# The score tiles of a step start with head 0 of their own key tile, and the copy of the finished values moves one exponential later

## What is computed

```python
# x (4, 512, 256), ctx_768 (4, 1601, 192); 16 heads of 16
q = (layernorm(x) @ Wq + bq).reshape(B, N, 16, 16)
k = (ctx @ Wk + bk).reshape(B, M, 16, 16)
v = (ctx @ Wv + bv).reshape(B, M, 16, 16)
attn = softmax(einsum('bnhd,bmhd->bhnm', q, k) / 4)
out = einsum('bhnm,bmhd->bnhd', attn, v).reshape(B, N, 256)
x = x + tanh(g_xattn) * (relu(out @ W1 + b1) @ W2 + b2)
x = x + tanh(g_ffn) * moe(layernorm(x))     # shared expert + top 2 of 8
```

## Time and profile before

| | |
|---|---|
| median of 3 runs | 1040.58 us (1040.33 to 1040.69) |
| the profiled execution | 1041.95 us, its span 1039.9 us |
| TensorE busy | 1021.9 us of the span |
| VectorE busy | 672.5 us |
| ScalarE busy | 610.9 us |
| attention steps | from about 61 us to about 720 us |
| granted TensorE clock, mean of the span | 0.997 of full speed |

### The profile page before, as it was taken

One profiled execution on the slowest core, in us unless ns is written; L12 is line 12 of the kernel. 1 busy time (PEld: TensorE's weight loads), 2 busy tenths in 40 slices (PEclk: granted clock), 3 DMA queues, 4 the chain that ended last, 5 costly groups with the idle time before them and its releaser, 6 DMA issues. The chain is left out here.

```text
span 1039.9 us, 15726 instructions
## 1 busy us (share of the span) xinstructions
PE 1021.9 (98%) x5777; PEld 555.7 (53%) x5777; DVE 672.5 (65%) x915; ACT 610.9 (59%) x1144; POOL 208.5 (20%) x217
## 2 busy tenths in 40 slices
PE   8899999999999999999999999999999999999998
PEld 6434445344445433444543353333676888888865
DVE  4998786896787798578788668711488222222326
ACT  3167777876677777577777768774365222222211
POOL 6129200009000003600000021020002233333310
PEclk9999999999999999999999999999999999999999
DMA  8263030430302402203033030011591111111207
GB/s 217 73 168 64 1 64 7 122 64 1 63 13 52 115 16 60 52 13 63 2 63 64 2 63 1 22 57 45 171 335 31 36 52 51 52 51 51 52 26 242
DMA packets 38281, 70.15 MB, mean 67 GB/s; under 512 B 6848, under 2 KB 23360, under 8 KB 38208
## 3 DMA queue, kind: packets, MB, share of 16 engines
q1 hardware_dynamic: 33072, 57.88, 21.3%
q0 software_dynamic: 3744, 10.23, 3.3%
q10 hardware_dynamic: 1392, 1.05, 0.4%
HBM read 33.70 MB, written 9.31 MB: 41 GB/s over the span
## 5 line engine op out<-in xcount | busy, mean ns | idle before, releaser
L1041 DVE TENSOR_REDUCE mpart<-gu_ps 128x2 f32<-128x1024 f32 x384 | 456.8, 1221 | 83.5 <-PE gu_ps L891 83.4
L743 ACT ACTIVATE probs<-ring_ps 128x512 f32<-128x512 f32 x816 | 433.1, 598 | 125.5 <-PE ring_ps L906 118.4
L906 PE MATMUL ring_ps<-qst,kst 64*128 64x512 f32 x816 | 224.8, 461 | 2.8 <-ACT probs L743 2.1
L921 PE MATMUL pv_ps<-probs,vp 128*32 128x512 f32 (+2 forms) x1664 | 222.7, 604 | 0.6 <-ACT osb L677 0.6
L906 PEld LDWEIGHTS ring_ps<-qst,kst 64*128 64x128 f32 x816 | 98.5, 180 | 207.6 <-ACT probs L743 117.8
L891 PE MATMUL gu_ps<-kst,qst 63*128 63x512 f32 (+1 forms) x1024 | 178.4, 396 | 6.6 <-DVE mpart L1041 5.4
L891 PEld LDWEIGHTS gu_ps<-kst,qst 63*128 63x128 f32 x1024 | 91.9, 186 | 66.7 <-DVE mpart L1041 42.3
L1261 ACT ACTIVATE h_sb<-gu_ps 128x512 f32<-128x512 f32 x55 | 32.8, 596 | 134.8 <-PE gu_ps L1415 134.7
L1468 DVE TENSOR_TENSOR h_sb<-h_sb,gu_ps 128x512 f32<-128x512 f32 x55 | 37.8, 687 | 113.3 <-ACT h_sb L1261 112.8
L302 POOL TENSOR_SCALAR veps<-mv 128x4 f32<-128x4 f32 x8 | 1.8, 231 | 531.9 <-DVE mv L1010 282.8
L1435 PE MATMUL y_ps<-wd,hT 128*128 x312 | 73.8, 380 | 0.0
(11 more groups left out here) (223 smaller groups left out, 1187.5 us busy)
## 6 DMA issues: line engine op xcount, KB each, us to landing
kst<-parts SPq DMA_DIRECT2D x45, 401.0 KB, 5.6
qst<-parts SPq DMA_DIRECT2D x48, 128.0 KB, 4.5
wgu<-in_WgT SPq DMA_DIRECT2D x16, 256.0 KB, 8.5
wgu<-in_WuT SPq DMA_DIRECT2D x16, 256.0 KB, 8.4
wd<-in_WdT SPq DMA_DIRECT2D x8, 512.0 KB, 9.6
wgu<-picked SPq DMA_DIRECT2D x8, 512.0 KB, 7.4
cold<-in_ctxT SPq DMA_DIRECT2D x3, 800.5 KB, 4.2
cold<-in_ctxT SPq DMA_DIRECT2D x6, 400.2 KB, 5.9
```

The costliest lines, as they stand in the source:

```text
L743: nc.scalar.activation(probs[0:w, m % NPB, h, :], bank_of(("st", idx))[0:w], ACT.Exp, scale=SCALE).then_inc(exp_done, 1)
L906: nc.tensor.matmul(bank_of(("st", idx))[0:w], kst[u % NKB][rows, h // 2, mt * P:mt * P + w], qst[u % NKB][rows, h // 2, :], start=True, st ...
L921: last = nc.tensor.matmul(pv_ps[32 * h:32 * h + c1 - c0, :], values[:, c0:c1], probs[0:w, m % NPB, h, :], start=(mt == 0), stop=(mt == MT ...
L1041: nc.vector.tensor_reduce(mpart[:, :, p, t, q], s_ps[:, n % NSP], AX.X, ALU.max).then_inc(s_free, 1)
```

## The change

The score tiles of a step become heads 0, 1, 2 and 3 of its own key tile, so each head 3 moves from the start of a step to the end of the one before. `lead` is 2 in every step. In unit 15 nothing is shifted beyond its first step: there the tiles ran one further ahead already, and still do. `take_pv` moves from the end of ScalarE's work in step mt = 0 to a place after the first exponential of step mt = 1. Ring and engines follow the same lists.

```diff
+LEADING = 2
...
-        first, last = (2 if m > MT * (UNITS - 1) else 0), (2 if m >= MT * (UNITS - 1) else 0)
-        return list(range(max(4 * m - 1 + first, 0), min(4 * m + 3 + last, 4 * MT * UNITS)))
+        first, last = (1 if m > MT * (UNITS - 1) else 0), (1 if m >= MT * (UNITS - 1) else 0)
+        return list(range(4 * m + first, min(4 * m + 4 + last, 4 * MT * UNITS)))
...
-        lead = 2 if m > 0 else 1
+        lead = LEADING
...
                 m = MT * u + mt
-                lead = 2 if m > 0 else 1
-                for idx in tiles_of(m)[:lead]:
+                lead = LEADING
+                for n, idx in enumerate(tiles_of(m)[:lead]):
                     exp(idx)
+                    if (mt, n) == (1, 0) and u > 0:
+                        take_pv(u - 1)
                 for job in jobs:
                     take(job)
                 for idx in tiles_of(m)[lead:]:
                     exp(idx)
-                if mt == 0 and u > 0:
-                    take_pv(u - 1)
```

## The result

The changed kernel takes 1042.71 us (median of 16 runs, 1042.24 to 1044.28) where the kernel before takes 1040.65 (16 runs, 1039.9 to 1041.98). The profiled execution took 1044.28 us, its span 1042.4. A step's time is that from the pv which opens it to the pv which ends it.

What follows compares the result with a forecast made beforehand. Bound: the round trip pv, position 1, its exponential, position 4, pv, 2.61 us a step. Losses 0.45 + 1.2 + 0.45 + 0.1 = 2.2, less rounding +2.1 us, gave 1042.7 us; range 1040.9 to 1043.5.

Steps and rivals of the forecast that it cites:

- The plain step: Steps without jobs, outside mt = 12, 0 and 1: still 2.61 us from pv to pv.
- the wait for the probabilities' buffer at position 1: Position 1's exponential, now a head 0, also waits for the pv two tiles back; over 0.3 us earlier, cost 0.
- the alternating halves of the array: Matmuls now alternate row halves throughout; gain only if same-half matmuls held each other up, none seen in the trace.
- C: Rival: pv wait at position 1 bites, each further 0.01 us costs 2 us; 0.14 together with other late waits.
- B: Rival: new order of heads is faster, 195 x 0.05 = 10 us, giving 1032 us; chance 0.07.
- The three terms: Copy's loss in step mt = 1: 0.45 us without a job, 1.2 with XT, 0.45 with K.
- the bank's wait: Step mt = 1 without a job: next pv needs the bank the copy empties, 0.05 to 0.06 us lost, eight times.
- the ring's: XT and K steps: position 4 waits for position 2's delayed exponential; 0.39 and 0.15 us lost each, three times.
- Rival A: Loss is absorbed: XT steps lose half, the others nothing; 1040.6 to 1042.0 us; chance 0.19.
- The start: V(0, 6) has to wait for the copy of V(0, 5): 0.1 us lost.
- The 65-key tiles: Both savings fall into mt = 12, near 2.49 us, mt = 0 back at 2.61; net 0.
- Unit 15: Six exponentials and the copy in one row on ScalarE, as before: 0.

Runs made afterwards that it cites:

- e6: The changed kernel once more, without an edit; 1042.43 us in one run.
- e1: Changed kernel with the copy put back to the end of step mt = 0, new order of heads kept; 1039.84 us, ratio 0.9988 to the kernel before.
- e2: Kernel before with only the copy moved behind the first exponential of step mt = 1, old order of heads kept; 1043.45 us, ratio 1.0021.
- e3: Changed kernel with the copy behind the second exponential of step mt = 1, not the first; 1046.44 us, ratio 1.0051 to the kernel before.
- e7: The version of e1 again, run beside e5 on one chip; 1039.65 us, ratio 0.9989 to the kernel before.
- e5: The version of e1 with the copy cut in two halves in the eight units without a job in mt = 1; 1039.0 us, ratio 0.9981.
- e4: Changed kernel with the copy put back to the end of step mt = 0 in unit 15 alone; 1041.77 us, ratio 1.0008.

## Why the prediction was right, point by point

**The plain step.** It was said to stay at 2.61 us; it takes 2.59 to 2.61, before and in both profiles of the changed kernel, and no plain step of e6 differs from its own of before by more than 0.02. With that the wait for the probabilities' buffer at position 1 and the alternating halves of the array are settled, the rivals C and B: each would have shown 195 times over. (Rival B's sum, 1042.7 - 195 x 0.05, gives 1033 and not 1032.)

**The copy.** The three terms, and what the eight, three and three steps show in the profiles:

| step mt = 1 | before | forecast | measured | forecast loss | measured loss |
|---|---|---|---|---|---|
| no job, 8 x | 2.69 to 2.70 | 2.76 | 2.75 to 2.76 | 0.45 | 0.5 |
| XT, 3 x | 3.19 to 3.20 | 3.59 | 3.58 to 3.59 | 1.2 | 1.2 |
| K, 3 x | 3.43 to 3.44 | 3.59 | 3.58 to 3.59 | 0.45 | 0.45 |

e1 and e2 show that these come from the copy alone, and e3 that the first is the bank's wait and the others the ring's, as the prediction put it. Rival A, that the loss is absorbed, falls.

**The start.** From the first score tile's load to that of V(0, 6): 57.43 - 56.67 = 0.76 us, where it was 56.50 - 55.84, or 0.67 before rounding. That is 0.09 lost, forecast 0.1.

**The 65-key tiles: the step that failed, in size.** The prediction put both savings into mt = 12 and their sum at zero. That holds where neither step has a job (2.49 and 2.59, 2.56 and 2.53). But where mt = 0 has a K or W2 job, it had gained nothing from its narrow position 1 and so had nothing to lose (unit 5: 5.99 us before, 5.98 after), while the mt = 12 ahead of it still gains from its narrow tiles; TensorE's job and not position 1's exponential then fills that step, by the rows. The rows of the pv that open and end the step mt = 12 of unit 4, changed kernel:

```profile
256.49 1.06 PE L922 MATMUL pv_ps<-probs,vp 128*32 128x512 f32 x8
...
262.41 1.06 PE L922 MATMUL pv_ps<-probs,vp 128*32 128x512 f32 x8
```

5.92 us; before:

```profile
254.96 1.06 PE L921 MATMUL pv_ps<-probs,vp 128*32 128x512 f32 x8
...
260.94 1.07 PE L921 MATMUL pv_ps<-probs,vp 128*32 128x512 f32 x8
```

5.98 us. Six units have such a pair of steps and gain 0.03 to 0.06 us each: 0.3 us that the sum lacks. So the term that the prediction put at zero was -0.3 us.

**Unit 15.** The two steps mt = 0 and 1 take 1.89 + 3.32 = 5.21 us in place of 2.55 + 2.56 = 5.11, and mt = 12 ahead of them 0.06 less: 0.04 where 0 was forecast. The copy does have as many exponentials ahead of it as before; it starts 4.41 us behind the pv that opens mt = 0 (4.35 before) and takes 0.66 (0.62). The fall of the clock in the first profile, 1.3 us in the step mt = 2, was not in the working at all.

**The sum.** 0.5 + 1.2 + 0.45 + 0.1 - 0.3 + 0.04, or 2.0 us, and the profiles say about 1.8: from the first pv to that of the step mt = 1 of unit 15 the kernel before takes 682.31 - 61.16 = 621.15 us, the changed one 684.89 - 62.08 = 622.81 and 684.36 - 61.48 = 622.88, so 1.66 and 1.73 more, and 0.09 at the start. The missing 0.2 us is spread over the other steps, 0.02 or less in nearly all of them. The medians differ by 2.06 us. The forecast of 2.1 was thus right in its parts to 0.3 us; that it hit the median to 0.01 us is luck, since falls of the clock move single executions by over 1 us, and the median with them. The spans of the first two profiles show it: their difference of 2.5 us is 0.8 from the first 10 us, 0.1 at the start, 1.7 in the steps, 1.3 from the clock in unit 15, less 1.4 behind the attention steps.

**What e1's gain is.** To the same pv e1 takes 681.78 - 61.44 = 620.34 us, 0.8 less than before: 0.4 of it in the steps mt = 0 and 1 of unit 15 (1.89 + 2.83 = 4.72 us where it was 5.11), since there one exponential fewer stands ahead of the copy (head 3 has moved out ahead and nothing was put in its place), and most of the rest in the mt = 12 steps. Its spans are 1037.9 and 1037.5, 2.0 and 2.4 us under that of before. Most of what is left lies behind the attention steps. From the last pv but one to the end of the span:

| | from that pv to the end | granted clock, 760 to 800 us |
|---|---|---|
| before | 1039.9 - 717.25 = 322.65 us | 0.91 |
| e2 | 1042.4 - 719.73 = 322.67 | 0.91 |
| changed | 1042.4 - 721.15 = 321.25 | 0.96 |
| e1 | 1037.9 - 716.72 = 321.18 | 1.00 |

The five other profiles, four at 0.96 and one at 1.00, have 321.2 to 321.3 too. So 1.4 us go with the long fall of the clock in that stretch, and none with the short one.

**What the medians hold.** Every execution of the experiments, and each of the changed kernel's 16, is on record with the mean clock of its whole span. Sorted by it, the time in us:

| | mean clock 0.997 | mean clock 0.998 or 1.000 |
|---|---|---|
| before | 26 executions, median 1041.8 | 22, 1040.3 |
| changed | 6, 1043.5 | 10, 1042.3 |
| e1 and e7 | 4, 1041.0 | 18, 1039.6 |
| e5 | 3, 1039.9 | 8, 1038.7 |

The kernel before has executions of both kinds, so its 1.4 us are no fixed part of the old order of heads. But its share of the slower kind is larger, and its median stands the higher for it: with like clock the changed kernel loses 1.7 to 2.0 us, e1 gains 0.7 to 0.8 us and not the 1.3 to 1.5 of the medians, and e5 gains 1.6 to 1.9. This is a comparison of executions and no experiment on the clock; a like mean can come from a fall in another place, and why the kernel before has the slower kind more often is open.

## What to carry to other kernels

When an operation moves on an engine that has idle time, ask not how much idle time there is but in which gap it stands: while ScalarE waited for the next score tile the copy cost a step 0.09 us; behind the first exponential it cost 0.06 to 0.39 us more. Find out for each kind of step which user of a ring waits for which earlier one; one job in between changed the partner, and with it the price from 0.06 to 0.39 us. A piece of work that just fails to fit a gap can be cut so that it does. And when two versions differ by 0.1 or 0.2%, compare their steps, and executions with a like granted clock, before their medians.

## What was not expected of the hardware

The TensorE clock fell to its lower level for a few us in one execution of a program and not in another. In the spans of nine profiles there are two places: unit 15 of the attention, in the first profile of the changed kernel, e3 and e4, and the stretch from 760 to 800 us, in all but the two profiles of e1's version. In unit 15 the wait of TensorE for the copy does not decide it: it fell with waits of 1.06, 1.55 and 0.57 us and stayed up with 1.06 (e6) and 0.56 (before). The step that it hit took 3.6 to 3.8 us and not 2.4, while a fall of the same length between 760 and 800 us cost nothing that the spans show. What decides this stays open; for comparing kernels that differ by 0.1% the steps of two profiles say more than their spans.

A pv released by a copy starts 0.14 us behind the copy's end, and its first weight load 0.11 (221.89 behind 221.78), where an exponential releases a score tile's load 0.05 us behind its own. The prediction took the 0.14 and the 0.05 from rows. The difference between the two loads is 0.06 us, as much as the copy's new place lost in the steps without a job.

Two ACTIVATEs on ScalarE in a row overlap: a copy of 0.60 us delays the next by 0.49. The Trainium skill (ScalarE: Activation LUTs, What ACT_TABLE_LOAD costs) gives an overlap of about 93 ns; here it is 0.11 to 0.12 (a copy of 0.59 or 0.60 us, the next start 0.47 to 0.49 behind its own). By its figure for an ACTIVATE without a pointer operand, 186 ns + 0.833 ns per element, half a copy would take 0.40 us, an estimate from that page; e5 shows 0.38.
